# Two-layer transformer on one core: causal attention with fewer inputs loaded ahead, statistics spread over ten places, a new order of work, and the first expert loads issued inside the last attention step

## The reference

```
x = x + L0_attn(layernorm(x))    # 16 heads of 16, causal, scores / sqrt(256)
x = x + L0_ffn(layernorm(x))     # gated MLP of 1024 + product-key experts (1024 rows of down/up_embed)
x = x + L1_attn(layernorm(x))    # rotary attention, one head of 128
x = x + L1_ffn(layernorm(x))     # mixture of 16 experts on 8 slices of 32 features
```

## Time and profile before

| | |
|---|---|
| median of three runs | 4173.62 us (4170.66 to 4175.27) |
| profiled execution | 4178.98 us, span in the profile 4177.1 us |
| causal attention | 0 to 1166 us |
| passage to the experts (`ln_scales`, `expert_weights`) | 1167 to 1186 us |
| PE busy over the span | 3942.8 us (94%) |
| DVE, ACT, POOL busy | 2784.8, 2640.7, 1554.6 us |

### The profile page before, as it was taken

One profiled execution on the slowest core, in us unless ns is written; L12 is line 12 of the kernel. 1 busy time (PEld: TensorE's weight loads), 2 busy tenths in 40 slices (PEclk: granted clock), 3 DMA queues, 4 the chain that ended last, 5 costly groups with the idle time before them and its releaser, 6 DMA issues. The chain is left out here.

```text
span 4177.1 us, 65914 instructions
## 1 busy us (share of the span) xinstructions
PE 3942.8 (94%) x23476; PEld 2362.2 (57%) x23476; DVE 2784.8 (67%) x5635; ACT 2640.7 (63%) x3262; POOL 1554.6 (37%) x1303
## 2 busy tenths in 40 slices
PE   7999999999968999999999989997999999999999
PEld 4455445554447788787887855554444444444444
DVE  7888778887668878878788545445545555554553
ACT  2566666666765545545455334444888888888888
POOL 3222222222334534435344211111555455455545
PEclk7999999999989999999999999999999999999999
DMA  7553444344142232332323210004666766667674
GB/s 180 129 113 75 103 99 104 91 112 111 29 121 76 61 106 77 80 103 61 109 74 84 84 35 1 1 1 106 154 154 154 163 146 154 154 148 159 148 160 99
DMA packets 205761, 429.98 MB, mean 103 GB/s; under 512 B 47584, under 2 KB 72560, under 8 KB 189056
## 3 DMA queue, kind: packets, MB, share of 16 engines
q1 hardware_dynamic: 193360, 411.56, 41.1%
q0 software_dynamic: 4160, 6.35, 0.6%
q10 hardware_dynamic: 7920, 7.87, 0.6%
HBM read 338.59 MB, written 87.03 MB: 102 GB/s over the span
## 5 line engine op out<-in xcount | busy, mean ns | idle before, releaser
L2202 ACT ACTIVATE gelu_out<-hidden,b_col 128x1024 f32<-128x1024 f32 x1024 | 1054.4, 1117 | 181.7 <-PE hidden L2125 176.0
L2185 POOL TENSOR_TENSOR combined<-combined,gated 128x512 f32<-128x512 f32 x480 | 621.5, 1295 | 647.4 <-DVE gated L2302 471.2
L663 DVE TENSOR_REDUCE maxima<-front_and_scoresT 128x1 f32<-128x512 f32 (+3 forms) x1280 | 725.6, 628 | 97.2 <-PE front_and_scoresT L471 61.7
L563 ACT ACTIVATE probsT<-front_and_scoresT 128x1024 f32<-128x1024 f32 (+3 forms) x768 | 599.4, 812 | 236.0 <-PE front_and_scoresT L498 229.8
L1127 POOL TENSOR_TENSOR pair_sums<-sims 128x1024 f32<-128x1024 f32 x256 | 482.9, 1902 | 668.3 <-DVEq L1259 412.5
L2302 DVE SCALAR_TENSOR_TENSOR gated<-out_bank,b_col,gates_spread 128x512 f32<-128x512 f32 x480 | 360.1, 750 | 511.5 <-PE out_bank L2133 482.6
L2125 PE MATMUL hidden<-slice_stack,w_stack 128*128 128x512 f32 x2048 | 622.9, 428 | 37.2 <-ACT gelu_out L2202 36.9
L1055 PE MATMUL dense<-xnT,dense_weights 128*128 128x512 f32 x2304 | 537.3, 395 | 12.7 <-ACT silu_down L1161 8.6
L2125 PEld LDWEIGHTS hidden<-slice_stack,w_stack 128*128 128x128 f32 x2048 | 354.5, 190 | 326.9 <-ACT gelu_out L2202 250.6
L2133 PE MATMUL out_bank<-gelu_out,w_sb 128*32 128x512 f32 x4096 | 517.5, 608 | 2.4 <-DVE combined L2302 2.2
L1055 PEld LDWEIGHTS dense<-xnT,dense_weights 128*128 128x128 f32 x2304 | 435.2, 190 | 112.8 <-ACT silu_down L1161 9.0
(11 more groups left out here) (205 smaller groups left out, 5063.3 us busy)
## 6 DMA issues: line engine op xcount, KB each, us to landing
gates_spread<-gate_scratch SPq DMA_DIRECT2D x512, 256.0 KB, 5.5
dense_weights<-dense_scratch SPq DMA_DIRECT2D x384, 256.0 KB, 2.8
stack_scratch<-split_parts SPq DMA_DIRECT2D x192, 256.0 KB, 3.2
slice_stack<-slice_scratch SPq DMA_DIRECT2D x128, 256.0 KB, 8.2
q_stack<-stack_scratch SPq DMA_DIRECT2D x64, 384.0 KB, 6.3
k_stack<-stack_scratch SPq DMA_DIRECT2D x64, 384.0 KB, 9.2
slice_scratch<-slice_parts SPq DMA_DIRECT2D x32, 512.0 KB, 5.9
out_x<-x_tiles ACTq DMA_DIRECT2D x15, 512.0 KB, 2.9
```

The source lines that it names most:

```text
L563: nc.scalar.activation(PT[:, i % NPT, 2 * pr:2 * pr + 2, at:BANK], R[:, low:high + 1:high - low, at:BANK], ACT.Exp, scale=SCALE).then_inc( ...
L663: nc.vector.tensor_reduce(dst, bank(k)[:, 0:parts * w].rearrange("p (a k) -> p a k", a=parts), AX.X, ALU.max)\
L2185: nc.gpsimd.tensor_tensor(CM[:, par, hc, :], CM[:, par, hc, :], Y[:, u % 2, :], ALU.add)\
L2202: nc.scalar.activation(GH[:, k % GHB, :, :], HP[k % HPB][:, :, :], ACT.Gelu, bias=b1c[:, n % E:n % E + 1])\
```

## The change

1. **Opening.** Batches 1 and 2 are loaded ahead, and 3 to 7 behind the first stack loads. The statistics in the opening cover 16 tiles instead of 32, and those of batches 3 to 7 come 4 tiles at a time behind the outputs of phases 1 to 10. The scales of batches 3 to 7 are made at phases 11 to 13 (before: 5 to 7 at 22 to 25).
2. **Order.** All five step strings are new; the opening string is the same.
3. **Passage.** Two tiles are shared between attention and experts (`EarlyWeights`): the three projection weights lie in one, xnT in the other. Behind the last value units SP loads the query weights and keys into the first, down_embed into the second. `ln_scales` is gone here: its operations stand in `expert_weights`, the first seven ahead of everything on DVE, the last five between the copies and the splits. The loads of up_embed and bd wait until PE has read the tiles in which they land. Four small tiles of the expert loop move into the shared one.

```diff
-    FIRST = ("mwwxmssmsmsmmsmvsmvsmvmxsmsmsmssmvsmmvsmmxxsmvxmtssmsosmsvmmxxvsmssmsmmsvvmxmmsvvsmsmmspssmvmvss"
+    FIRST = ("wmmmwsmsmsmsssvxsmsvmsmvmxsxmsmvsmsmsvmsmvmstxxmsmvsmsmsmsxxmvmsmvssmsmvmssvvmsoxmmvssmssmmmpmmp"
...
-        wq = sb("wq_sb", [P, DC, 2, HS, HH])
-        wk = sb("wk_sb", [P, DC, 2, HS, HH])
-        wv = sb("wv_sb", [P, DC, H, HS])
+        wq, wk = (early.small[:, i, :].rearrange("p (c f d h) -> p c f d h", c=DC, f=2, d=HS) for i in range(2))
+        wv = early.small[:, 2, :].rearrange("p (c h d) -> p c h d", c=DC, h=H)
-        XT = sb("xnT", [P, DC, T])
+        XT = early.rows
-        STATS_AT = {3: 5, 4: 6, 5: 7}
-        LN_AT = 4 * 6
-        LN = [(0, KT), (KT, 5 * KT), (5 * KT, B * KT)]
-        AHEAD = range(1, 5)
-        LATER = range(5, B)
+        AHEAD = range(1, 3)
+        LATER = range(3, B)
+        LN = [(0, KT), (KT, 3 * KT), (3 * KT, B * KT)]
+        TILES_AT = 4
+        STATS_AT = {1 + k: 3 * KT + TILES_AT * k for k in range((B - 3) * KT // TILES_AT)}
+        LN_AT = 12
...
+                if n + 2 == NS:
+                    sp.wait_ge(freed[True], NFREE[KF["w", NS - 1, 1]])
+                    early.load(sp)
...
-                if unit[0] == "o" and unit[1] % 4 == 0 and unit[1] // 4 in STATS_AT:
-                    stats(STATS_AT[unit[1] // 4])
+                if unit[0] == "o" and unit[1] in STATS_AT:
+                    for t in range(STATS_AT[unit[1]], STATS_AT[unit[1]] + TILES_AT):
+                        if t % KT == 0:
+                            dve.wait_ge(later_in[t // KT - 1], 16)
+                        tile_stats(nc, X, STATS, t)
...
             def _(sp):
-                later_loads(sp)
+                small_loads(sp)
                 for b in range(NB):
                     sp.wait_ge(copied_dve, copies(NC + b))
                     sp.dma_start(dense.scratch[b], DP[:, b, :, :, :].bitcast(F32)).then_inc(dense.down_stored, 16)
+                sp.wait_ge(filled, NC + NB)
+                up_load(sp)
...
-                pe.wait_ge(loaded, 16 * (DC + 3))
+                pe.wait_ge(early.prep_in, 16 * (DC + 2))
...
+                pe.wait_ge(early.down_in, 16)
                 for b in range(NB):
...
             def _(dve):
+                ln_begin(nc, dve, STATS, MEAN, var_ready)
                 nc.vector.memset(KB[:, :, :, :], 0.0).then_inc(zeroed, 1)
...
+                ln_end(nc, dve, STATS, RS, var_ready, sd_ready)
                 for b in range(NB):
...
             def _(act):
+                ln_root(nc, act, STATS, var_ready, sd_ready)
                 act.wait_ge(zeroed, 1)
```

More of the change, by code:

```diff
@@ L37, in tile_stats, with ln_begin, ln_root, ln_end @@
     nc.vector.bn_stats(STATS[:, t, :], X[:, t, :])
-def ln_scales(nc, STATS, MEAN, RS, tag, loads=None, consts=None):
+def ln_begin(nc, dve, STATS, MEAN, var_ready):
+    VE, DM = STATS[:, :, 0], STATS[:, :, 3]
+    nc.vector.tensor_tensor(MEAN[:, :], STATS[:, :, 1], STATS[:, :, 4], ALU.add)
+    nc.vector.tensor_tensor(DM, STATS[:, :, 1], STATS[:, :, 4], ALU.subtract)
+    nc.vector.tensor_tensor(VE, STATS[:, :, 2], STATS[:, :, 5], ALU.add)
+    dve.drain()
+    nc.vector.tensor_scalar(MEAN[:, :], MEAN[:, :], 0.5, None, ALU.mult)
+    nc.vector.tensor_tensor(DM, DM, DM, ALU.mult)
+    nc.vector.tensor_scalar(VE, VE, 1.0 / D, EPS, ALU.mult, ALU.add)
+    dve.drain()
+    nc.vector.scalar_tensor_tensor(out=VE, in0=DM, scalar=0.25, in1=VE, op0=ALU.mult, op1=ALU.add).then_inc(var_ready, 1)
+def ln_root(nc, act, STATS, var_ready, sd_ready):
+    act.wait_ge(var_ready, 1)
+    nc.scalar.activation(STATS[:, :, 1], STATS[:, :, 0], ACT.Sqrt).then_inc(sd_ready, 1)
+def ln_end(nc, dve, STATS, RS, var_ready, sd_ready):
+    VE, SD, R0, R1 = (STATS[:, :, i] for i in (0, 1, 4, 2))
+    dve.wait_ge(sd_ready, 1)
+    dve.wait_ge(var_ready, 1)
+    nc.vector.reciprocal(R0, SD)
+    dve.drain()
+    nc.vector.tensor_tensor(R1, R0, R0, ALU.mult)
+    dve.drain()
+    nc.vector.tensor_tensor(R1, R1, VE, ALU.mult)
+    dve.drain()
+    nc.vector.tensor_scalar(R1, R1, -0.5, 1.5, ALU.mult, ALU.add)
+    dve.drain()
+    nc.vector.tensor_tensor(RS[:, :], R0, R1, ALU.mult)
+def ln_scales(nc, STATS, MEAN, RS, tag, loads=None):
     with ExitStack() as ctx:
-        VE, DM, SD, R0, R1 = (STATS[:, :, i] for i in (0, 3, 1, 4, 2))
         var_ready = ctx.enter_context(nc.semaphore(f"var_ready_{tag}"))
@@ L340, in _ @@
             load_batch(sp, 0, x_in, 2)
-            for w, dst in ((Wq, PT[:, 0, 0, :]), (Wk, PT[:, 0, 1, :]), (Wv, wv[:, :, :, :].rearrange("p c h d -> p (c h d)"))):
+            for w, dst in ((Wq, PT[:, 0, 0, :]), (Wk, PT[:, 0, 1, :]), (Wv, early.small[:, 2, :])):
                 for c in range(DC):
@@ L710, in _ @@
                     ln_end(1)
[L711 to L713 removed]
+                if unit[0] == "o" and unit[1] in STATS_AT:
[3 more added lines that the diff above has]
+                        tile_stats(nc, X, STATS, t)
+                if unit == ("o", LN_AT - 1):
                     ln_begin(2)
@@ L878, in expert_ffn @@
         SD = sb("silu_down", [P, NB, TM])
-        GS = sb("silu_gate", [P, 2, TM])
         HT = sb("hiddenT", [P, FB, TM])
-        T8 = sb("top_pairs", [P, TT * H, TOPK])
-        TD = sb("top_less_max", [P, TT * H, TOPK])
+        small = early.small[:, :, :].rearrange("p i n -> p (i n)")
+        GS = small[:, 0:2 * TM].rearrange("p (i t) -> p i t", i=2)
+        T8, TD = (small[:, 2 * TM + i * P:2 * TM + (i + 1) * P].rearrange("p (g k) -> p g k", k=TOPK) for i in range(2))
+        bdr = small[:, 2 * TM + 2 * P:2 * TM + 2 * P + D]
         NMX = sb("neg_max", [P, TT * H])
```

125 lines of the change are left out of this document (57 added, 68 removed).

## The result

The changed kernel took 4215.93 us (median of 6 runs, 4210.97 to 4222.48), the kernel before on the same chip 4172.14 us (6 runs, 4158.43 to 4185.74). The ratio is 1.0107, with a 95% interval of 1.0084 to 1.0130: 44 us slower. The forecast was 4190 us with a range to 4204, so the sign was right and the size less than half of what came. One execution of experiment 3's version took 5392.89 us at a granted clock of 0.65, and the ratio there leaves it out.

The account below looks back on a forecast made before the run. PE was taken to bound steady attention, its waits being paid in full. Boundary +18, clock +4, step 0 +4, statistics -2, opening -1, passage -5.9 gave +17 on 4178.98, or 4196; median forecast 4190 us, range 4159 to 4204.

Parts of the forecast that it names:

- The sum: Whole kernel: all terms add to +17 us on the profiled 4178.98, or 4196; forecast 4190 for the median.
- What bounds the kernel: Steady attention: PE is busy 98.9 of 100 us, so whatever makes it wait in steps 1 to 13 is paid in full.
- The even-to-odd boundary: Behind even steps 2 to 12: row maxima delay unit 3's stores and stack loads; six longer PE waits, +18 us, bounds 0 and +24.
- the stack loads come 3.5 us later: Even-to-odd steps: unit 3's stores begin 6.9 us behind its projection's start, not 3.4, so each wait grows 3.0 us.
- The clock behind the waits: Behind the six boundary waits: a lowered PE clock costs +4 us, bounds 0 and +15.
- The x loads: Step 0: two more late batches ahead of the second group's row maxima cost at most +1 us, the opening's upper bound.
- Step 0 to step 1: Start of step 1: PE arrives 3.4 us sooner but scores start no sooner; +4 us, bounds 0 and +6.
- Opening: Start of the kernel: the saved statistics are off the path, the first stores land a little sooner; -1 us, bounds -3 and +1.
- Passage: Attention to experts: down_embed is already loaded, so the experts' first work starts sooner; -5.9 us, bounds -8.5 and -3.5.
- Statistics: DVE in attention: groups of four tiles replace whole batches, one burst less; -2 us, bounds -11 and +5.5.
- (c): Whole kernel: every wait lowers the clock for good (+15), the loads meet traffic (+24); +34, 4207 us; chance 0.11.

Follow-up runs that it names:

- experiment 3: Changed kernel with the order strings, x loads and statistics of the kernel before, so only the passage stays; 0.9991 of the kernel before, 4174.88 us.
- new order mended: Changed kernel with the maxima turned earlier in even steps and step 0, and four late x batches behind step 0's row maxima; 1.0013 of before, 4187.60 us.
- run 4: Changed kernel; in even steps from 2 on SyncE issues unit 3's stores and stack loads ahead of the row maxima; 1.0087 of the kernel before, 4215.15 us.
- run 2: Changed kernel with the five old order strings, everything else of the change kept; 1.0001 of the kernel before, 4176.06 us.
- run 5: Changed kernel with one letter moved: in even steps the second turn of the maxima stands ahead of units 0 to 3; 1.0060 of before, 4206.62 us.
- run 1: Kernel before with all five step strings exchanged for the new ones and nothing else of the change; 1.0101 of the kernel before, 4220.08 us.
- run 7: Changed kernel, maxima turned earlier in step 0, four late x batches behind its row maxima: new order, even steps also turned early, 1.0013; old order 0.9972.
- experiment 7: Changed kernel, four late x batches behind step 0's row maxima, early turn there: new order with early even-step turns 4187.60 us; old order 4166.65 us.

## Why the prediction was right in sign and wrong in size

- **The sum.** Forecast +17, measured +32.7 between the two profiles. The boundary gave 6.5 more than forecast, the row maxima of step 0's second group 6.7, the clock 5.1 (9.1 for 4), other idle time 3.7 less. The other 11 us up to the 44 of the medians are in no profile; the busy times of PE below make the clock the likely place, which is not shown.
- **What bounds the kernel: right as far as the profile goes.** PE's longer idle time (28.0) and its longer busy time for the same matmuls (9.1) make up the 37.1 us in attention.
- **The even-to-odd boundary: the mechanism right, the term too small.** It gave +18 with an upper bound of +24; it measured +24.5 in the change and +29.5 with the order alone. The step that failed, in size, is "the stack loads come 3.5 us later", with "the wait grows by 3.5 - 0.5 = 3.0 us". The stores came 4.4 us later and the wait grew by 4.1: the row maxima hold SyncE 3.5 us from one issue to the next on average, up to 4.3, not the 3.0 of the row that I took the earlier trace rows, and my 2.7 us from unit 2 to unit 3 were 2.5 in the boundary shown (725.65 to 728.12). The section of the Trainium skill that the prediction names (DMA: Bandwidth & Descriptors, "Anatomy of one DMA") gives its 2.0 us for DMAs issued through GpSimd, while SyncE issues these. The estimate of 2.6 us that rests on it was further from the measured 3.5 than the row. PE's way was right (I had 18.5 from the projection's start; 16.5 behind its end is 18.3). The upper bound was wrong as well: traffic was to be its reason, and the loads did not get slower.
- **The clock behind the waits: the size wrong.** I counted 10 to 20 us for six waits and then took +4, since one short wait had cost nothing. Around the wait of 5.65 us the clock stands at 0.50 (1.2 GHz) for the 20 us from 605 to 625, 16 of them behind the wait. PE was busy 9.1 us longer than in the profile of before. But that profile is at the upper end of the six with the old order (1078.05 to 1088.22, mean 1083.2), and the three with the long stack waits have 1097.27, 1103.92 and 1108.07: 14 to 25 us above that mean. The count stood in the text; the choice went against it. But a count that goes by the length of the waits does not hold in these runs either: the new order mended, with short waits, has 1096.69, and run 4, with the longest, 1081.69 (table at the end).
- **The x loads: missed.** The five later batches ahead of step 0's row maxima had a bound of +1, and a wait of 6.71 us stood there. I had looked at when the data is needed, and not at the small store queued behind it. Three batches with the new order made a wait of 3.31 us, five with the old order one of 6.50, three with the old order none.
- **Step 0 to step 1: the number right, partly by luck**, 8.23 us for the 8 to 9 forecast. I had PE come 3.4 us sooner behind unit 3's start and the scores no sooner. PE came 1.1 us sooner (17.4 instead of 18.5), and the scores could start 2.4 us later (25.6 instead of 23.2, from 155.80 to 181.41), mostly since the stack loads were issued 9.8 us behind unit 3's start and not 8.1.
- **Opening: right** (-1.2 for -1). **Passage: right** (-5.3 for -5.9, which by its own numbers, 1183.1 to 1177.4, is -5.7; with the passage alone the time is 3.8 us lower, with an interval of 7 us to each side).
- **Statistics: right within its bounds.** The long waits for DVE's maxima (5.4 us in four) became 1.2 in three, the short ones 3.0 instead of 1.4; together 2.6 us less for the -2 forecast. With the old order (run 2) the same statistics left 7.9 us of these waits, more than the 6.8 of before, so the gain is not the statistics' alone. The remaining fall of idle time, above all 3.8 us of waits for ACT, had no term.
- **The probability.** The case that came is (c), "every wait lowers the clock for good, the loads meet traffic", 4207 with a chance of 0.11: right that the clock falls behind all six waits, wrong on the traffic, and still 9 us short.

Not settled: why the transfers of the early turn (run 5) take 11.5 us instead of 10.5, why PE's clock is lower behind the boundary waits of the new order, short or long, but less so in run 4, and where the 11 us are that the two profiles do not show. Moving the x loads in the old order brought 14 us where the wait had 6.5; that is within the interval and the run-to-run differences of the clock, about 10 us.

## What to carry to other kernels

An order table sets not only what PE does next, but what stands next to what in the queue of the engine that issues the DMAs. For each transfer that PE waits for, list what is issued ahead of it on that queue, together with any wait for a landing among them, and price the move by the largest gap seen in that place and not by one sample. And give the clock a term of its own with a wide range: with the new order PE was busy 10 to 25 us longer than the mean of the old order in five of six profiles, and the length of the waits did not tell how much.

## What the runs showed of the hardware

- SyncE waits for a store of the row maxima to land before it issues the next DMA. From issue to next issue this takes 1.5 us when nothing is ahead (706.04 to 707.51), 2.6 to 4.3 behind a unit's stores (731.05 to 734.36 is 3.3), 8.7 to 11.1 behind the stack loads of run 4's six boundaries (740.44 to 751.28 is 10.8), and 10.0 behind five x loads (112.46 to 122.43).
- Issuing itself can block: five x loads held SyncE for 24.52 us in a row, three for 18.10 in the kernel before, but four of them, issued 26 us after the first one (88.65, 114.83), for 5.54.
- The clock does not follow the length of the waits. Behind the end of each of the six boundary waits I took the granted clock of the next 20 us; the last column is PE's busy time in attention:

| | length of the six waits | clock of the next 20 us, mean (range) | PE busy in attention |
|---|---|---|---|
| before | 0.3 to 2.9 | 0.96 (0.85 to 1.00) | 1088.22 |
| after | 3.6 to 6.8 | 0.71 (0.58 to 0.90) | 1097.27 |
| order alone (run 1) | 5.6 to 6.8 | 0.65 (0.59 to 0.91) | 1103.92 |
| new order mended (run 7) | 1.6 to 2.5 | 0.77 (0.57 to 1.00) | 1096.69 |
| SyncE's order alone (run 4) | 7.5 to 9.3 | 0.88 (0.85 to 0.90) | 1081.69 |

The last row's boundary of step 8, to set beside the row at 586.06 in experiment 7:

```profile
754.53:774.53 20.00, 20.00 (x161) 11.67 (x162) 12.05 (x24) 12.35 (x18) 4.08 (x7) 0.85 0.57 120
```

What makes the difference the runs do not show.
